# A four-stage sequence kernel on one NeuronCore: the mixer's second conv tile, z's split and the last group's output product change places

## The reference

```python
proj = einsum('bld,pd->blp', x, in_proj_w)          # gate 4096 | hbc 6144 | dt 64
xBC  = silu(conv_bias + causal 4-tap conv of hbc)   # x | B | C, 8 groups of 128
state = state * exp(dt * A) + dt * x * B            # per head, step by step
y    = (state . C) + x * D
y    = y * rsqrt(mean(y * y over the group) + eps) * norm_weight * silu(gate)
out  = einsum('bli,di->bld', y, out_proj_w)
```

## Time and profile before

| | us |
|---|---|
| median of 3 runs (1332.19 to 1333.8) | 1332.53 |
| the profiled execution | 1333.64 |
| its span, first to last instruction | 1331.9 |
| busy PE / DVE / ACT / POOL | 1239.0 / 926.7 / 691.6 / 658.7 |
| a loop group (group 4: 529.90 to 647.82) | 117.92 |
| last group to the next layer's first product in p_gb (883.72 to 1015.5) | 131.8 |

### The profile page before, as it was taken

One profiled execution on the slowest core, in us unless ns is written; L12 is line 12 of the kernel. 1 busy time (PEld: TensorE's weight loads), 2 busy tenths in 40 slices (PEclk: granted clock), 3 DMA queues, 4 the chain that ended last, 5 costly groups with the idle time before them and its releaser, 6 DMA issues.

```text
span 1331.9 us, 22035 instructions
## 1 busy us (share of the span) xinstructions
PE 1239.0 (93%) x6680; PEld 966.3 (73%) x6690; DVE 926.7 (70%) x1734; ACT 691.6 (52%) x1042; POOL 658.7 (49%) x707
## 2 busy tenths in 40 slices
PE   5999999999999999999999999998878999889976
PEld 4777777776777777777777777776666777667764
DVE  5786677667667766766776676677766655569995
ACT  3675666566656656675666567555523333222220
POOL 5056546654744665475465456543663434343330
PEclk9999999999999999999999999999989999999996
DMA  5111011011101201110010110010003233131100
GB/s 174 45 49 34 1 51 48 18 33 48 32 1 32 64 16 32 48 30 3 32 64 16 32 48 25 9 37 1 22 27 107 83 95 98 44 94 35 56 16 24
DMA packets 44233, 57.52 MB, mean 43 GB/s; under 512 B 10117, under 2 KB 21159, under 8 KB 43929
## 3 DMA queue, kind: packets, MB, share of 16 engines
q1 hardware_dynamic: 44185, 56.92, 14.0%
HBM read 49.95 MB, written 6.96 MB: 43 GB/s over the span
## 4 chain that ended last, share of the span: by engine, by line
PE 68%; DVE 11%; issue 9%; ACT 7%; POOL 2%; DMA 1%; DVEq 1%; SPq 1%; ACTq 0%; POOLq 0%
PE p_d L94 14%; PE p_d L98 7%; PE p_gate L94 6%; PE p_tile L94 5%; PE p_in L1092 4%; PE p_x L1100 4%; DVE conv L702 3%; PE p_y L1121 3%; PE p_gate L98 3%; PE p_tile L98 2%; PE t_p_a L1872 2%; PE p_y L94 2%; ACT L612 2%; PE t_p_c L1940 2%; PE p_in L94 2%
## 5 line engine op out<-in xcount | busy, mean ns | idle before, releaser
L702 DVE SCALAR_TENSOR_TENSOR conv<-p_tile,conv_taps,conv 128x511 f32<-128x511 f32 x189 | 141.4, 748 | 46.2 <-ACT conv L573 31.2
L812 DVE TENSOR_TENSOR em<-em,p_gb 128x512 f32<-128x512 f32 x128 | 82.1, 682 | 65.7 <-ACT em L612 65.7
L702 DVE SCALAR_TENSOR_TENSOR conv<-p_d,conv_taps,conv 128x511 f32<-128x511 f32 (+2 forms) x99 | 73.9, 747 | 65.8 <-ACT conv L573 61.9
L94 PE MATMUL p_d<-wr_hi,zt_hi 128*128 128x512 f32 x248 | 101.1, 408 | 13.1 <-DVE wr_lo L740 7.9
L94 PE MATMUL p_tile<-xn_hi,wc_hi 128*128 128x512 f32 x252 | 110.1, 437 | 0.8 <-DVE halo L706 0.8
L578 ACT ACTIVATE xbc<-conv 128x512 f32<-128x512 f32 x96 | 60.6, 631 | 94.2 <-DVE conv L710 57.9
L516 POOL TENSOR_TENSOR squares<-squares 128x256 f32<-128x256 f32 x64 | 47.7, 746 | 122.2 <-ACT squares L635 122.2
L485 POOL TENSOR_TENSOR x_w<-xs,head_g 128x512 f32<-128x512 f32 x56 | 59.2, 1057 | 98.3 <-ACT xs L606 97.8
L94 PE MATMUL p_gate<-xn_hi,wr_hi 128*128 128x512 f32 x248 | 104.2, 420 | 0.0
L635 ACT ACTIVATE squares<-y 128x512 f32<-128x512 f32 x64 | 40.5, 633 | 119.8 <-DVE y L845 116.4
L94 PE MATMUL p_tile<-xn_lo,wc_hi 128*128 128x512 f32 x252 | 98.5, 391 | 0.0
(11 more groups left out here) (361 smaller groups left out, 3511.8 us busy)
## 6 DMA issues: line engine op xcount, KB each, us to landing
...
```

The lines of the kernel that those rows point to most:

```text
L94: pe.matmul(out, lhs(k)[0], rhs(k)[n], start=(start and k == 0 and n == 0), stop=False)
L702: ve.scalar_tensor_tensor(out=conv[:, s, sh:], in0=p[:, 0:HALF - sh], scalar=conv_w[:, bass.ds(g, 1), j, tap], in1=conv[:, s, sh:], op0=AL ...
L812: ve.tensor_tensor(m, m, gm.unsqueeze(1).broadcast_to([P, HG // 2, P]), ALU.mult)\
```

## The change

1. **Banks.** The second conv tile goes into p_gate instead of p_d1 (`bank_of`). The gate tile of steps 0, 1, 4 and 5 goes into p_tile (`gate_bank`), that of the others stays in p_gate. So L1072 waits for no taps. Conv tiles 1, 2 and 4 wait for the Silu of the gate tile made before them (`s_sg`), tiles 0, 3 and 5 for taps.
2. **Taps.** The second tile's remaining taps move behind the next step's B work on DVE (`left`), its Silu behind that step's exponentials on ACT; in steps 1, 4 and 5 one more tap stays in its own step.
3. **z.** `z_round(n)` and `z_rest(n)` move from the next step into their own: on ACT between the squares and the gate's Silu, on DVE behind `residual`.
4. **Residual and variance.** Outside the tail, `sum_rows(n - 1)` on PE moves behind the second conv tile, `variance(n - 1)` on DVE behind the state, `norm` on POOL behind the y add, and `residual(n - 1)` from the middle of the step to behind z.
5. **Output weights.** POOL makes the rests of the third and fourth (`out_rest`: a multiply by the scale, a subtraction), DVE those of the first two. ACT rounds the third and fourth first, before `tile_in` of the second tile.
6. **Last group, steps 4 to 7.** `sum_rows(n - 1)` and `out_product(n - 1)` come right behind L1072, before the row transposes; the row sum has a column of p_gate (`ss_bank`); on DVE `variance` comes before the row norms, `residual` and `row_stats` before the state. After the last step the first products of the next layer, the last row sum and output product are reordered likewise.

The diff's core:

```diff
+    def ss_bank(last, c):
+        return p_gate[:, 0:1] if last and CH <= c < NC else p_gb[:, 3 * P:3 * P + 1]
+    def gate_bank(c):
+        return p_tile if c % CH < 2 else p_gate
     def bank_of(j):
-        return (p_tile, p_d1)[j in (1, 3)]
+        return (p_tile, p_gate)[j in (1, 3)]
-    VE_LO = list(range(TILES + KT, WT))
-    POOL_LO = list(range(TILES + KT))
+    VE_LO = [OUT, OUT + 1]
+    POOL_LO = list(range(OUT)) + ["scaled", OUT + 2, "scaled", OUT + 3]
+    ROUNDED = [OUT + 2, OUT + 3, OUT, OUT + 1]
...
 # POOL
+                if c == 0:
+                    for w in (OUT + 2, OUT + 3):
+                        out_rest(g, w)
-                if not (isinstance(g, int) and n == 0) and not tail:
-                    norm(n - 1, (c - 1) % 2)
                 if c > 0:
                     pool.tensor_tensor(y[:], y[:], x_d[:], ALU.add).then_inc(s_txd, 1)
+                if not (isinstance(g, int) and n == 0) and not (last and c >= CH):
+                    norm(n - 1, (c - 1) % 2)
...
+        def out_rest(g, w):
+            raw = w_raw[:, w % RAW, :]
+            scale = norm_w[:, bass.ds(g, 1), w - OUT].broadcast_to([P, D])
+            pool.wait_ge(s_whi, hi_count(g, w))
+            pool.tensor_tensor(raw, raw, scale, ALU.mult).then_inc(s_wlo, 1)
...
+            pool.tensor_tensor(lo_of(w), raw, hi_of(w).bitcast(F32), ALU.subtract).then_inc(s_wlo, 1)
...
 # ACT
-                for tile in left:
-                    tile_silu(*tile)
...
-                if not first:
-                    z_round(n - 1, p_y)
...
-                for tile in now:
+                for tile in left + now:
                     tile_silu(*tile)
...
                 act.activation(squares[:], y[:], ACT.Square).then_inc(s_sq, 1)
+                z_round(n, y_bank(last, c))
                 made = gate_tile(g, last, c)
                 if made:
-                    wait(act, s_z, n)
-                    gate_silu(CH + n, made[1], made[2])
+                    gate_silu(CH + n, made[1], made[2], gate_bank(c))
...
 # PE
-                for _, tg, j, hf in left:
-                    pe.wait_ge(s_tap, tapped(tg, hf, j) + TAPPED[hf])
...
-                if not first and not tail:
+                if tail:
+                    pe.wait_ge(s_sg, LAST + 1)
+                    wait(pe, s_v, n - 1)
+                    sum_rows(n - 1, ss_bank(last, c))
+                if not first:
                     pe.wait_ge(s_e, 2 * n + 1)
                     out_product(n - 1, p_d0)
-                    pe.wait_ge(s_m, 2 * (n + 1))
-                    sum_rows(n - 1)
...
                 pe.wait_ge(s_m, 2 * (n + 1))
-                if tail:
-                    sum_rows(n - 1)
+                if not first and not tail:
+                    sum_rows(n - 1, ss_bank(last, c))
...
-                if tail:
-                    if c < NC - 1:
-                        pe.wait_ge(s_e, 2 * (n + 1))
-                    out_product(n - 1, out_bank(last, c))
```

142 lines of the change are left out of this document (73 added, 69 removed).

## The result

The changed kernel takes **1323.1 us** (median of 4, 1320.9 to 1324.11) against 1332.46 for the kernel before (4 runs, 1332.19 to 1333.8): ratio 0.9924, interval 0.9912 to 0.9937. It is faster, by 9.4 us or 0.8%, and the interval leaves 1 out. The prediction said 1303.3, 1292 to 1318: the direction was right, the gain a third of the forecast, and the time outside the range. Run again beside the last experiments it took 1324.3.

The account below looks back on a forecast made before the run. PE is busy nearly throughout the loop, so only its 5.15 us standing per group can be won. Loop 16.8, group 0 1.5, last group 2.0, tail 8.9: 29.2 off 1332.53 gives 1303.3 us, range 1292 to 1318.

Parts of the forecast that it names:

- the bound is DVE's chain: Last group, steps 4 to 7: PE's work fits beside DVE's chain, which sets step length; 8.9 us won.
- What comes in steps 0 and 1: Each group: POOL's two out-weight splits take 4.7 us ahead of the norm's power; out product starts 0.65 us sooner.
- the wait that is renamed: Start of step 1: L1072 still starts at about 310.95, now waiting for the residual, about 1 us a group.
- DVE in step 1: Loop step 1: DVE nearly full, PE waits 0.4 at step 2; steps 1 and 2 together win 1.5 us.
- the rule in hand: A two-SBUF-input DVE instruction contends with a GpSimd instruction reading SBUF; the loser blocks for the whole of the other.
- Steps 5 and 6: Loop steps without out weights: of 0.76 + 0.66 us standing, 1.3 us won per group.
- Group 0 and steps 1 and 2 of the last group: Outside the loop groups: 1.5 us won in group 0, 2.0 us in the last group's steps 1 and 2.
- Rival (c): The tail gives nothing, as row sums and variance wait for POOL: 20.3 us won, 1312; chance 0.13.
- (b): POOL and DVE slow each other in steps 0 and 1, which win nothing: 18.2 us won, 1314; chance 0.20.
- (a): More is won: splits don't contend, 40 us won, 1292; a denser tail could also speed its clock; chance 0.15.
- (d): Slower: conv tiles wait for the gate's Silu after steps 0, 1, 4, 5; about 1337 if 2.5 us late; chance 0.04.

Follow-up runs that it names:

- the version with both loop edits: Changed kernel, with POOL's sums of squares ahead of the state's decay product (except last four steps) and the norm's power between the two out-weight splits: 1302.65 us.
- Run 1: Changed kernel, with POOL's sums of squares issued ahead of the state's decay product in all steps but the last four: 1314.4 us.
- run 7: Changed kernel, with POOL's sums of squares ahead of the rows' power and the state's decay product in the last four steps: 1318.0 us.
- the last run: The version with both loop edits, plus, in the last four steps, squares first, PE and DVE queues reordered, e_cum ahead of the large exponentials: 1289.8 us.

## Why the prediction was wrong

The standing time of PE and its names were read rightly, and in the loop the floor was where it said: 5.15 us of standing per group, of which the version with both loop edits wins 4.5. Two terms failed: the time of DVE's chain in step 1, which took the instructions at their length alone (2.8 us a group forecast, 1.5 measured), and "the bound is DVE's chain" in the tail (8.9 forecast, nothing measured). Step by step:

- **"What comes in steps 0 and 1"**: right on the wait that is renamed (1.38 us against about 1, the power ending 0.1 us from where it was put; step 1 17.34 against 17.2). The splits on DVE were priced at 1.5 and took 0.78 and 0.95 in the loop, so that the wait on `wr_lo` went altogether, and the mask behind them starts 19.2 us into the group instead of the 20.6 forecast.
- **"DVE in step 1"**, the first wrong term. It had "variance, y, z 1.6" and "three short" taps in 2.5 for the left tile. z took 1.56 instead of 0.70, and the left tile 5.1 instead of 2.5. Expected wait at step 2: 0.4; measured 1.36. Steps 1 and 2 together won 0.65 where 1.5 was forecast, and step 3 lost 0.5 where nothing was forecast. That is 1.35; with 0.2 less in steps 5 and 6 and 0.2 more in steps 0, 4 and 7 it makes the difference between 2.8 and 1.5 per group, 8 us over six groups. Run 1, which moves POOL's work away from z, gave 1.36 back. The prediction had the rule in hand and asked it only about `out_rest` in step 0, where it "would change nothing in this sum". It did not ask what stands beside the same instruction in the steps behind, once the power has moved behind y's add: L483 does, next in POOL's order.
- **Steps 5 and 6**: 1.3 forecast, 1.1 measured. The same stretch costs 0.5 there (15.85 and 13.13 against 15.61 and 12.84 in run 1); that only 0.2 are missing is because the floor lies lower than the forecast put it.
- **Group 0 and steps 1 and 2 of the last group**: 1.5 forecast and 1.1 measured for the one; 2.0 forecast and 2.7 measured for the other, then given back whole in step 4. The step that failed is calling a shorter step a gain without asking who sets the start of work in the next stretch: DVE's end of step 3 did, 61.8 us into the group, before as after, and through it POOL's power and sums.
- **"The bound is DVE's chain"**, the second wrong term, 8.9 us. DVE's chain was counted with its own hand-overs, and PE's part was laid beside it "in the gap in front of the row transposes". That gap was 2.0 to 2.2 us in steps 4 to 6 (3.2 in step 7); the product put into it takes 3.05, and took 4.3 to 4.6 there, at the lower clock. Everything that y needs (row transposes, inter product, intra product) was then behind it on PE: the inter product starts 3.2 us later in step 5 and 4.5 later in step 6. The old order had the out product behind the intra product, beside y and z, where PE's next step waited 0.5 to 1.1 us for DVE. For steps 4, 5, 6 and 7 the forecast was 0.7, 2.3, 1.5 and 4.4 won; measured were 3.2 lost, 0.6 won, 0.25 lost and 2.4 won, and 1.6 of that went in the next stage's clock. Rival (c) has the outcome; of its reason ("`sum_rows` now heads PE's queue and the variance DVE's; both wait for POOL") the waits are there, 4.61 us in step 4 and 1.57 in step 6, but with the first removed (run 7) the tail's trace was as long as before. Which of the three chains, PE's, POOL's or DVE's, holds each step of the changed kernel stays open; that DVE's alone does not, in the length forecast, is shown by the steps of 13.2 to 15.6 us with DVE busy 8.5 to 11.0.
- **Rivals and range.** (b), the stretching of POOL and DVE, happened, but hardly in the instructions it named: its price of 1.5 for each of POOL's four met only the last (1.04, 1.29, 1.05, 1.61 in the group shown), and the loss sat on z and the halo taps instead. (b) and (c) were each worked out alone, 1314 and 1312. They lie in different stretches, and both came true in effect: (b)'s 18.2 without the tail's 8.9 are 9.3 us won, 1323.2, and 1323.1 was measured. That the two numbers meet so closely is luck, since parts of both were off; but a range that ends at the single rivals leaves out their sum. (a) showed its other half in the experiments: in the last run, with a shorter chain, the tail did speed itself up (PE busy 8.80 us in step 5 where it had been 10.11). (d) did not occur: PE waited for the gate's Silu once in the whole span, 1.4 us.
